# A graph layer with a routed FFN on one core: 24 blocks' expert rows fetched as eight runs of 64 rows and summed by TensorE, in place of row gathers

## The reference, cut to what matters

```python
x = x + _L0_gnn_ref(_layernorm(x, axis=-1), W_self, W_neigh, b, src, dst)   # sums over the edges
x = x + _L0_ffn_ref(_layernorm(x, axis=-1)[None], ...)[0]
# in _L0_gnn_ref
agg = jax.ops.segment_sum(feat[src], dst, num_segments=n)
out = feat @ W_self + (agg / jnp.maximum(deg, 1.0)[:, None]) @ W_neigh + b
# in _L0_ffn_ref
logits = jnp.einsum('bsd,de->bse', xn, Wr) + br
top_vals, top_idx = jax.lax.top_k(logits, K)          # K = 2
w = jax.nn.softmax(top_vals, axis=-1)
for e in range(E):
    h = jax.nn.gelu(jnp.einsum('bsd,dh->bsh', xn, W1[e]) + b1[e], approximate=False)
    y = y + (jnp.einsum('bsh,hd->bsd', h, W2[e]) + b2[e]) * w_full[..., e, None]
```

## Time and profile before

| | us |
|---|---|
| median of 3 runs | 1268.87 |
| lowest and highest run | 1264.01 and 1272.49 |
| the profiled execution's own time | 1265.15 |
| its span, first to last instruction | 1263.1 |
| PE busy | 1095.5 (87%) |
| PE's weight loads busy | 971.6 (77%) |
| POOL busy | 942.5 (75%) |
| DVE busy | 865.6 (69%) |
| ACT busy | 435.7 (34%) |

### The profile page before, as it was taken

One profiled execution on the slowest core, in us unless ns is written; L12 is line 12 of the kernel. 1 busy time (PEld: TensorE's weight loads), 2 busy tenths in 40 slices (PEclk: granted clock), 3 DMA queues, 4 the chain that ended last, 5 costly groups with the idle time before them and its releaser, 6 DMA issues.

```text
span 1263.1 us, 22169 instructions
## 1 busy us (share of the span) xinstructions
PE 1095.5 (87%) x6356; PEld 971.6 (77%) x6357; DVE 865.6 (69%) x2812; ACT 435.7 (34%) x812; POOL 942.5 (75%) x980
## 2 busy tenths in 40 slices
PE   0479999989987999999899898987989887988987
PEld 0368888979976888998788787776778776877977
DVE  7886766777676767768767675855667764655447
ACT  7723322323433334434434443433224312211131
POOL 7677777777667777777777777777777777777774
PEclk9999999999998999999999898998999999999989
DMA  9999987866556476666756665656687668766766
GB/s 351 328 317 377 301 294 262 287 199 211 179 166 202 146 253 198 221 199 207 213 183 199 187 191 185 195 162 209 188 259 221 211 213 275 227 219 210 230 206 227
DMA packets 163993, 287.57 MB, mean 228 GB/s; under 512 B 25632, under 2 KB 93344, under 8 KB 163744
## 3 DMA queue, kind: packets, MB, share of 16 engines
q1 hardware_dynamic: 115280, 153.36, 36.5%
q0 software_dynamic: 45696, 124.88, 32.6%
q10 hardware_dynamic: 2896, 7.87, 1.7%
HBM read 228.81 MB, written 57.20 MB: 226 GB/s over the span
## 4 chain that ended last, share of the span: by engine, by line
PE 54%; POOL 13%; DVE 12%; issue 9%; DMA 7%; SPq 2%; ACT 1%; DVEq 0%; POOLq 0%; ACTq 0%
PE bank L966 17%; PE bank L1042 13%; POOL ring L689 11%; PE bank L1068 8%; PE bank L1076 5%; PE bank L995 3%; PE bank L954 3%; PE bank L997 2%; DMA ring<-feature_table,src_sb 2%; DMA heap<-in_x 1%; PE bank L1092 1%; DVE heap L1480 1%; POOL pair L711 1%; DVE agg L1323 1%; PE bank L1103 1%
## 5 line engine op out<-in xcount | busy, mean ns | idle before, releaser
L689 POOL DMA_INDIRECT ring<-feature_table,src_sb x756 | 743.1, 983 | 248.1 <-issue 218.9
L966 PE MATMUL bank<-ring,onehot 128*128 128x257 f32 x1544 | 393.3, 399 | 100.0 <-issue 57.9
L966 PEld LDWEIGHTS bank<-ring,onehot 128*128 128x128 f32 x1544 | 302.0, 199 | 157.9 <-issue 109.9
L868 ACT ACTIVATE heap<-heap 128x512 f32<-128x512 f32 x139 | 87.8, 632 | 335.2 <-DVE heap L1480 335.2
L1480 DVE TENSOR_TENSOR heap<-bank,b_sb 128x512 f32<-128x512 f32 x139 | 95.9, 690 | 145.0 <-PE bank L1042 77.4
L1068 PE MATMUL bank<-heap 128*128 x728 | 182.5, 395 | 13.7 <-DVE y_out L1489 7.9
L1042 PE MATMUL bank<-row_t,heap 128*128 128x128 f32 x1456 | 179.1, 277 | 0.7 <-DVE heap L1480 0.6
L1042 PEld LDWEIGHTS bank<-row_t,heap 128*128 128x128 f32 x1456 | 173.4, 194 | 2.6 <-issue 1.1
L1068 PEld LDWEIGHTS bank<-heap 128*128 128x128 f32 x728 | 137.2, 196 | 31.8 <-issue 14.7
L1323 DVE SCALAR_TENSOR_TENSOR agg<-bank,in_first,agg 128x257 f32 x196 | 94.4, 482 | 96.5 <-PE bank L966 62.9
L1281 DVE TENSOR_TENSOR onehot<-iota,target 128x512 f32<-128x512 f32 x196 | 134.2, 685 | 7.1 <-DVE xf L1340 4.8
(11 more groups left out here) (193 smaller groups left out, 1250.6 us busy)
## 6 DMA issues: line engine op xcount, KB each, us to landing
heap<-in_w SPq DMA_DIRECT2D x139, 512.0 KB, 5.0
expert_out<-empty_row SPq DMA_DIRECT2D x68, 256.0 KB
ring<-feature_table,src_sb POOLq DMA_INDIRECT x756
row<-expert_rows SPq DMA_DIRECT2D x91, 128.5 KB, 4.3
xf<-in_x SPq DMA_DIRECT2D x49, 128.0 KB
ff<-feature_table SPq DMA_DIRECT2D x49, 128.0 KB
expert_out<-inside SPq DMA_DIRECT2D x46, 128.0 KB
expert_out<-y_out SPq DMA_DIRECT2D x45, 128.0 KB
```

Source lines behind the costliest of these rows:

```text
L689: pool.indirect_dma_start(group_row(t, i)[:, 0:D], None, x if t < RAW else table, bass.IndirectOffsetOnAxis(src_sb[:, k:k + 1], 0)).then_i ...
L868: act.activation(hid[s], hid[s], ACT.Gelu).then_inc(S.gelu, 1)
L966: last = pe.matmul(bank[t % 2][:, 0:D + 1], onehot[:, q, i, :], group_row(t, i), start=(i == 0), stop=(i == GT - 1))
```

## The change

It concerns the 24 blocks that are merged beside the main loop; the other 18 keep their gathers.

- Each row of `rows_tab` and `expert_out` gets one more column with a tag, the node's number plus one. DVE writes it when a block is placed (`slots`) and copies it in `weighted`.
- For the first 25 places in the order of the blocks DVE keeps where each expert's rows begin (`starts`).
- In step t of a merge SP reads the eight starts and issues eight plain DMAs, 64 rows of 257 numbers each, into one buffer of 128 partitions by 4 (`fetch_runs`). In step t + 1 DVE compares the tags with the block's node numbers, which gives four one-hot matrices of 128x128 (`hot_runs`). In step t + 2 PE multiplies the four by the fetched rows into `result_b` (`sum_runs`) and DVE adds that to x1 (`add_runs`). In step t + 3 SP stores the block (`store_added`).
- There is one buffer for the fetched rows: the next block's fetch, which has its place in step t + 2, waits on SP until PE has multiplied. A tile's store waits on SP until the rows last asked for have landed.
- All of the last 18 merges now wait until the groups are summed.
- If in one of the 24 blocks an expert has more than 64 rows, a counter makes the kernel do everything again in a slow way.

```diff
+            def fetch_runs(i):
+                n, tiles, at = merges[i]
+                if i:
+                    sp.wait_ge(runs_sum, X_IN + i)
+                sp.wait_ge(main.rows_set, rank[n] + 1)
+                tiles_put(hold, main, tiles_stored[0])
+                for e0 in range(0, NE, 4):
+                    firsts = load_values(mybir.EngineType.SP, starts[0:1, i, e0:e0 + 4], NE * CAP, **unchecked)
+                    for e, first in enumerate(firsts, e0):
+                        p0, h = e * RUN % P, e * RUN // P
+                        sp.dma_start(runs_in[p0:p0 + RUN, h, :], expert_out[bass.ds(first, RUN), :]).then_inc(runs_landed, 16)
+            def store_added(i):
+                sp.wait_ge(runs_added, X_IN + i + 1)
+                sp.dma_start(nodes(out, NB - 1 - merges[i][0]), x1_of(main, merges[i][0])).then_inc(d_out, 16)
...
             def store_rows(S, j):
...
+                if S.planned and runs_fetched[0]:
+                    sp.wait_ge(runs_landed, X_IN + 16 * NE * runs_fetched[0])
...
                 for j in tiles_in(t, "store"):
                     store_rows(main, j)
-                for i in merges_in(t, -1):
-                    store_merged(i)
+                for i in merges_in(t):
+                    fetch_runs(i)
+                for i in merges_in(t, -3):
+                    store_added(i)
...
             def take_rows(i):
-                if k >= STAGE_BUFFERS:
-                    pool.wait_ge(summed, NG)
-                else:
+                pool.wait_ge(summed, NG)
+                if k < STAGE_BUFFERS:
+                    pool.wait_ge(runs_sum, X_IN + STAGE_MERGES)
                     pool.wait_ge(x_in[k], 16 * (merge_use[i] + 1))
...
                 for n in routed_in(t, "scatter"):
                     scatter_rows(main, n)
-                for i in merges_in(t):
-                    take_rows(i)
...
             def results(S, j):
...
                     result_free(S.unit(j))
+                    if runs_summed[0]:
+                        pe.wait_ge(runs_added, X_IN + runs_summed[0])
...
+            def sum_runs(i):
+                pe.wait_ge(runs_landed, X_IN + 16 * NE * (i + 1))
+                pe.wait_ge(runs_hot, X_IN + i + 1)
+                result_free(units_done[0])
+                if i:
+                    pe.wait_ge(runs_added, X_IN + i)
+                halves = NE * RUN // P
+                for h in range(halves):
+                    last = pe.matmul(result_b[:, 0:D], run_hot[:, h, :], runs_in[:, h, 0:D], start=(h == 0), stop=(h == halves - 1))
+                last.then_inc(runs_sum, 1)
...
+            def hot_runs(i):
+                dve.wait_ge(runs_landed, X_IN + 16 * NE * (i + 1))
+                if i:
+                    dve.wait_ge(runs_sum, X_IN + i)
+                link(dve.tensor_scalar(tags[:, :], runs_in[:, :, D], float(-P * merges[i][0] - 1), None, ALU.add))
+                halves = NE * RUN // P
+                dve.tensor_tensor(run_hot, iota[:, :].unsqueeze(1).broadcast_to([P, halves, P]),
+                                  tags[:, :].unsqueeze(2).broadcast_to([P, halves, P]), ALU.is_equal).then_inc(runs_hot, 1)
+            def add_runs(i):
+                x1 = x1_of(main, merges[i][0])
+                dve.wait_ge(runs_sum, X_IN + i + 1)
+                dve.tensor_tensor(x1, x1, result_b[:, 0:D], ALU.add).then_inc(runs_added, 1)
```

More of the change, by code:

```diff
@@ L165, in build @@
     STAGE_MERGES = len([at for n, tiles, at in merges if at is not None])
-    merge_buffer = [i % STAGE_BUFFERS if i < STAGE_MERGES else (i - STAGE_MERGES) % MERGE_BUFFERS for i in range(len(merges))]
+    merge_buffer = [None if i < STAGE_MERGES else (i - STAGE_MERGES) % MERGE_BUFFERS for i in range(len(merges))]
     merge_use = [merge_buffer[:i].count(merge_buffer[i]) for i in range(len(merges))]
@@ L311, in build @@
         first_pass = sb("first_pass", [1, NE])
-        late = sb("late", [1, len(MERGE_CLAIMS) + 4])
+        late = sb("late", [1, len(MERGE_CLAIMS) + 5])
+        tags = sb("tags", [P, NE * RUN // P])
         row = [sb(f"row{s}", [P, R]) for s in range(XR)]
         row_t = [sb(f"row_t{s}", [P, DK, P]) for s in range(2)]
-        in_scratch = NT // D
-        y_out = [inside[:, s * D:(s + 1) * D] for s in range(in_scratch)] + [sb(f"y_out{s}", [P, D]) for s in range(in_scratch, XY)]
+        in_scratch = NT // Y
+        y_out = [inside[:, s * Y:(s + 1) * Y] for s in range(in_scratch)] + [sb(f"y_out{s}", [P, Y]) for s in range(in_scratch, XY)]
         small_in, dst_in, src_in, w2_in = (sem(n) for n in ("small_in", "dst_in", "src_in", "w2_in"))
@@ L1132, in _ @@
                     product(main, n)
+                for i in merges_in(t, -2):
+                    sum_runs(i)
                 for u in early_in(t, "result"):
@@ L1390, in slots @@
                                         places[:, :].unsqueeze(1).broadcast_to([P, 2, NE]), ALU.mult))
+                if S.planned and rank[n] <= STAGE_MERGES:
+                    dve.tensor_copy(starts[0:1, rank[n], :], places[0:1, :])
+                if S.planned:
+                    dve.tensor_scalar(rows[s][:, :, D + 1], iota_p[:, 0:1].broadcast_to([P, 2]), float(P * n + 1), None, ALU.add)
                 dve.tensor_tensor(placed_so_far[:, :], placed_so_far[:, :], both[s2][:, :], ALU.add).then_inc(S.acc_set, 1)
@@ L1599, in _, with unit_sums @@
                     x1_sums(main, n)
[L1600 to L1607 removed]
+                def unit_sums(now):
+                    for u in early_in(t, "sum"):
+                        if (dense_at["result"][u] == t) == now:
+                            if u % NE == 0:
+                                dense_shares(DENSE_BLOCKS[u // NE], 3 * (u // NE))
+                            if DENSE_BLOCKS[u // NE] == LAST - 1:
+                                dve.wait_ge(added, t - 1)
+                            early_sum(u)
+                    for j in tiles_in(t, "weigh"):
+                        if (tile_at["result"][j] == t) == now:
+                            weighted(main, j, of_tile.pop(j))
+                unit_sums(False)
+                for i in merges_in(t, -2):
+                    add_runs(i)
+                unit_sums(True)
                 if 1 <= t < NG:
```

105 lines of the change are left out of this document (63 added, 42 removed).

## The result

The changed kernel took **1374.26 us** (median of 4 runs, 1372.17 to 1385.08), and the kernel before took 1266.44 us beside it (median of 4 runs, 1260.91 to 1272.49). The ratio is 1.087, with a 95% interval of 1.080 to 1.093: slower by 108 us. The profiled execution is the slowest of the four, 11 us over the median.

A forecast was written before the change was run, and what follows sets the result against it. POOL bounds the merge stretch by its indirect DMAs, with PE close behind; after the change PE would bind. 1265.15 + 41.5 + 30.5 - 26.4 + 19 + 3 = 1332.8, so 1333 us, range 1276 to 1378.

The forecast's parts named there:

- SP becomes the bound: Rival: in the merge stretch a merge's round on SP takes 18 us, not 15.5; 1364 us, chance 0.17.
- POOL: Steps 140 to 187: POOL is the bound by its count of indirect DMAs; 48 fewer relieve it of 60.5 us.
- (a) The matmuls: Merge stretch: four added 128x256 matmuls a block on PE, 24 blocks, +41.5 us.
- (b) the hand-over: Merge stretch: PE's result waits until DVE has added the sums, 1.27 us in each of 24 merges, +30.5 us.
- (c) the waits gone: Merge stretch: PE's waits for gathers ahead of group matmuls disappear, -26.4 us.
- The gap ahead of L1109: Sign: PE idle about 1.3 us ahead of the tile's result after each of the 24 sums.
- SP's lateness: Merge stretch: tile's rows or expert matrix sometimes land late for PE, 0.8 us a merge, +19 us (0 to 98).
- the 10 given as a sign: Sign: SP's fetches take about 10 us from the sum's end to the last landing; much more or less means wrong size.
- The clock: Merge stretch: PE still pauses at each merge, so clock dips stay; 0, with -9 us kept for the range.
- The longer rows: Rows of 257 in place of 256 numbers add 0.4% to DMAs beside other work; 0.
- The end: Kernel's end: POOL's last merges now wait for PE's last group, +3 us (0 to 6).
- The rival that the Trainium skill bears on: Rival: POOL's relief in the merge stretch reaches the end, 60.5 us less with +3 at the end; 1208, chance 0.05.

The follow-up runs named there:

- runs 3: Changed kernel with only four of the eight fetches a merge, the other four experts' rows left out of the sums: 1321.95 us, ratio 1.045.
- run 7: Changed kernel with four of the eight fetches (other experts' rows left out) and the sums in another PSUM bank: 1296.72 us, ratio 1.024.
- run 4: The kernel before, with only the zeros filling the expert output table written in 1028-byte pieces in place of 1024: 1275.01 us, ratio 1.0065.
- Run 12: run 10 with four of the eight fetches issued on ACT's queue in place of SP's, nothing left out: 1297.50 us, ratio 1.025.
- run 6: Changed kernel with expert_out filled by the same bytes in 1024-byte pieces in place of 1028-byte ones: 1370.11 us, ratio 1.083.
- run 10: Changed kernel with SP's order loads, fetches, store, the sums in another PSUM bank and 1024-byte fill, nothing left out: 1324.04 us, ratio 1.046.
- run 11: run 10 with one of the four summing matmuls a block, three quarters of the rows fetched but not summed: 1320.88 us, ratio 1.044.

## Why the prediction was right, and where it was not

1374 us lies in the range of 1276 to 1378, and slower was given 0.82. But the **forecast's mechanism was wrong**, and that the number is inside the range is owed to the width that the rivals gave it. It said that PE would be the bound, with a little lateness of SP, 1333 us. What happened is the rival to which 0.17 was given: SP becomes the bound at about 18 us a round, priced at 1364 us (18.6 were measured). Step by step, for steps 140 to 187:

- *POOL.* Right. It was the bound by its count of indirect DMAs: with 43 fewer in the stretch it waits 127.4 us for PE, and the 26.4 us ahead of the groups are 0.5.
- *(a) The matmuls*, +41.5, *(b) the hand-over*, +30.5, *(c) the waits gone*, -26.4: these gave 381.4 us for PE's stretch, without lateness. Where SP is in time, runs 3 and 7 measure it: 386.5 us with the hand-over, 354.4 without, against 381.4 and 350.9 by the sum. The gap ahead of L1109 was 1.11 us in the round shown, and 29.0 us in all, for 30.5. PE's part was priced to within 5 us.
- *SP's lateness*, +19. **This is the step that failed**: 437.2 - 381.4 = 56 us. SP's round was taken at 15.5 us, just under PE's 15.9, and was 18.6. By parts, forecast and then measured: the fetches 5.4 and 5.7; waiting for them to land 4.5 and 0.4, since loads stand in between; other issues 3.5 and 6.6, because four were counted, one step's, where two steps have seven; waiting for stores to land 2.1 and 4.2, because the 2.1 came from the end of the kernel, where little else moves; PE's sum 0 and 1.5; empty rows 0 and 0.2. So the issues and the wait for stores were too small by 5.2 us together, and the fetch's landing too large by 4.1. Even without the wait for PE that is 17.1 us: SP's ring, and not PE's, was the longer.

  The other half of the step held: in the round shown the tile's rows land at 1210.27, 11.3 us after the sum's end at 1198.96, where the forecast had 11.2, and a fetch takes 8.7 us from the sum's end (1214.28) to the last landing (1222.98), not much less than the 10 given as a sign. PE, though, was ready for the rows 9.6 us after the sum, not 11.2.

  Behind the sizes stands an error of method: the working took a margin of 0.4 us between two rings that share SP as slack. Where they wait for each other in turn, as here, a late part of one can be carried into the other; the 1.5 us a round of waiting for PE are its trace, but no run measures that alone.
- *The clock*, 0 (-9 in the range). Wrong in sign. PE did the same 1,900 records in 351.3 us at a granted clock of 0.93 that took it 327.4 us in run 7 at 0.98, 24 us less. In the changed kernel the clock stood at half (1.2 GHz) for 64.9 us of the stretch, with PE busy in 49.2 of them; in run 7 for 17.1, with 13.0. Half of the difference in busy time, 18 us, is the cost of half clock; the other 6 are not accounted for. It is a stretch in which PE pauses at every merge (idle 85.9 us, against 27.0 in run 7). The Trainium skill ("TensorE: Matmul & The Clock Gate", Part 1, the clock gate) has the throttle released by activity; the two rows agree with that, read the other way round: where PE waited more, its work went slower too. So SP's lateness comes with two parts, idle time and a lower clock. Against the 400.4 us that the forecast had for the stretch, 36.8 are missing: 19.2 us of PE's busy time (351.3 for 332.1) and 17.6 of its idle time.
- *The longer rows*, 0. Wrong: 8 us at the end (run 4), about 10 us at group 140. The 0.4% was worked out on bytes, and a DMA engine is not busy by bytes alone: in 100 to 300 us the DMAs were already busy for 0.85 of the time, and 1028-byte pieces made that 0.96 (run 4). Runs with 1028-byte fill reached group 140 late by 2.6 to 18.3 us (eight of them, mean 10.5), runs with 1024-byte fill by -2.6 to 3.5 (five, mean 0.9). The changed kernel's profiled execution has the largest of these, 8 us over their mean, which may be most of the 11 us by which it is over the median.
- *The end*, +3. The mechanism was right, POOL waits for PE's last group; the size was +1.2 from that group's end on, inside the 0 to 6.

By the medians: +108 is about 8 for the fill (run 4), which belongs to the steps ahead of 140, and some 100 for the stretch. The rival that the Trainium skill bears on ("Perfetto Trace Analysis", DMA Optimizations: spread DMAs over the issuing engines where descriptor generation binds) was no gain as the change applied it, since it took 48 DMAs off POOL and put 192 on a queue that is in order and full of waits. Run 12 shows the rule at work on that queue: half of the fetches on ACT's gave 26.5 us.

**What stays open.** How the 56 us part into SP's issues, landings and lower clock is known only by the runs' differences, since the three move together. What makes a store's landing longer in the stretch than at the end of the kernel was not tested. Whether the landing waits themselves could be dropped was not tried: the runs read up to 64 rows for each expert whatever the count, so later stores write rows that a fetch may read. And whether the even fill helps the changed kernel's total is not shown (run 6: 4 us, within the intervals).

## What to carry to other kernels

When work moves from an engine that is the bound to a queue that is in order, don't add up that queue's instructions and compare the sum with the new bound; follow one item around each closed ring of waits (issue, landing, consumer, release, next issue), count every issue that the queue makes in a round (seven here beside the fetches, not four), and take the landings from the busy stretch. If two rings come out within a few per cent of each other, as here (15.5 and 15.9 us), the margin is no slack. To learn which ring binds, take away part of each suspect by itself: three quarters of PE's summing were worth 3 us (in run 10, with SP's order changed already), half of SP's fetches 52 us (in the changed kernel).

## What the runs showed of the hardware that was not expected

- DMAs of 64 rows take SP longer to issue than DMAs of 128 rows. The changed kernel's fetches, its loads of a tile's rows, which go the same way with 128 rows, and, of the kernel before, the empty rows, eight in a row the other way (ns min/median/max):

```profile
L533 SPq DMA_DIRECT2D pairs<-expert_out x192: 468/468/1376, 836.9 to 1283.5; - x192
L575 SPq DMA_DIRECT2D row<-expert_rows x91: 332/343/780, 297.6 to 1315.6; - x91
```

```profile
L525 SPq DMA_DIRECT2D expert_rows<-empty_row x8: 332/338/509, 1040.2 to 1044.5; - x8
```

  Neither the direction nor eight in a row explains the 468. The tile stores with the fetches' row length, 1028 bytes, and 128 rows take 356 ns (median). The number of rows is what is left; no run changes it alone.

- Pieces of 1028 bytes in place of 1024 cost the queues far more than 0.4% where they are nearly full. SP's queue from 100 to 300 us, first of the kernel before, then of the changed kernel (packets, MB, share of the 16 engines' time):

```profile
q1 hardware_dynamic: 29177, 35.39, 53.6%
```

```profile
q1 hardware_dynamic: 29051, 34.76, 62.7%
```

  The same number of packets and slightly fewer bytes take 17% more of the engines' time (62.7 / 53.6). In run 4, where only the fill differs, it is 63.2% for 29,518 packets and 35.43 MB. In the changed kernel an expert matrix of 512 KB, loaded meanwhile, lands after 8.9 us in place of 5.3 (medians).
- Taking 20 us of work from PE where it does not bind went with a lower granted clock: 0.93 (run 11) against 0.96 (run 10) in the stretch of the profiled executions, and over the whole kernel 0.953 to 0.961 against 0.962 to 0.970 in the four runs of each.
